# Key products of a recurrence round in four banks instead of two, and the last turn of outputs moved between two projections

## The reference

```
qkvz = einsum('bsd,od->bso', layernorm(x), W_qkvz)        # q, k, two v, two z for each of 16 heads
q, k, v = silu(causal_conv4(q, k, v)); q, k = rmsnorm(q), rmsnorm(k)
g = cumsum over the chunk; decay[i,j] = exp(g_i - g_j) for i >= j
M = where(i > j, einsum('cd,md->cm', k * beta, k) * decay, 0)
T = inverse(eye + M)                                      # 64 x 64, unit lower triangular
v_c, k_cumdecay = T @ (v * beta), T @ (k * beta * exp(g))
for each chunk:                                           # the recurrence
    attn  = (q @ k.T) * decay
    v_new = v_c - k_cumdecay @ state
    out   = (q * exp(g)) @ state + attn @ v_new
    state = state * exp(g_last) + (k * exp(g_last - g)).T @ v_new
h   = norm_w * rmsnorm(out) * silu(z)
s   = einsum('bsf,df->bsd', h, W_out)                     # summed over the heads
y   = x + s * silu(feed_forward(layernorm(x)))
```

## Time and profile before

| what | value |
|---|---|
| median of 3 runs | 2178.77 us (2178.72 to 2179.42) |
| profiled execution: its own time / its span | 2178.21 us / 2176.4 us |
| PE busy (matmul) | 2070.3 us, 95% of the span |
| DVE busy | 1597.4 us, 73% |
| POOL busy | 1670.5 us, 77% |
| ACT busy | 1192.7 us, 55% |
| chain that ended last | PE 49%, DVE 33%, ACT 9%, issue 6%, POOL 2% |
| granted TensorE clock, mean | 0.992 |

### The profile page before, as it was taken

The page is one execution under the profiler, slowest core; times in us unless marked ns, Lnnn a source line. Parts: engine busy times, 40 slices in busy tenths (PEclk is TensorE's granted clock), DMA queues, the critical chain, the costliest instruction groups (busy, mean ns, idle before and its releaser), DMA issues.

```text
span 2176.4 us, 75165 instructions
## 1 busy us (share of the span) xinstructions
PE 2070.3 (95%) x31952; PEld 1578.1 (73%) x31952; DVE 1597.4 (73%) x3083; ACT 1192.7 (55%) x2757; POOL 1670.5 (77%) x1774
## 2 busy tenths in 40 slices
PE   3799999999999999999999999999999999999998
PEld 2677777777777777777777777777777777776644
DVE  5777777778777777778777777778777777776322
ACT  3565556655665556655665556655665556654211
POOL 2788888888888888888888888888888888888200
PEclk9899999999999999999999999999999999999999
DMA  2211101111121101121121102111121102111100
GB/s 87 58 41 39 48 17 41 39 48 34 36 48 39 47 16 44 39 49 34 36 48 39 47 14 46 39 48 34 36 48 39 48 11 48 39 39 45 45 15 20
DMA packets 57485, 86.31 MB, mean 40 GB/s; under 512 B 7488, under 2 KB 30144, under 8 KB 57152
## 3 DMA queue, kind: packets, MB, share of 16 engines
q1 hardware_dynamic: 57152, 81.50, 15.2%
HBM read 76.92 MB, written 4.55 MB: 37 GB/s over the span
## 4 chain that ended last, share of the span: by engine, by line
PE 49%; DVE 33%; ACT 9%; issue 6%; POOL 2%; DMA 0%; DVEq 0%; POOLq 0%; SPq 0%; ACTq 0%
DVE cacc L1024 11%; PE ps_two L452 8%; PE ps_state L425 5%; PE ps_p L615 4%; DVE terms L1126 3%; PE ps_p L501 3%; ACT qg L799 3%; PE ps_state L639 3%; PE ps_p L680 3%; PE ps_p L623 3%; PE ps_p L588 3%; PE ps_p L452 2%; PE ps_p L739 2%; ACT L790 2%; PE ps_two L539 2%
## 5 line engine op out<-in xcount | busy, mean ns | idle before, releaser
L1411 POOL TENSOR_SCALAR Kg<-idx_s,lutb 128x134 f32<-128x134 int32 x480 | 356.3, 745 | 27.1
L1372 POOL TENSOR_TENSOR Sd<-St,el 128x512 f32<-128x512 f32 x192 | 201.3, 1048 | 196.9 <-DVEq L1266 196.9
L1245 DVE TENSOR_SCALAR Vn<-ps_p,bR 128x128 f32<-128x128 f32 x512 | 165.9, 349 | 189.8 <-PE ps_p L588 114.1
L425 PE MATMUL ps_two<-xnT,w_qkv 128*128 128x256 f32 x1024 | 235.7, 383 | 17.7 <-DVEq L1029 17.7
L1024 DVE SCALAR_TENSOR_TENSOR cacc<-ps_state,cw,cacc 128x1022 f32<-128x1022 f32 (+2 forms) x192 | 244.2, 1272 | 7.9 <-ACT cacc L772 3.1
L1024 DVE SCALAR_TENSOR_TENSOR cacc<-ps_two,cw,cacc 128x1022 f32<-128x1022 f32 (+2 forms) x192 | 244.8, 1275 | 5.3 <-DVE cacc L1024 0.5
L680 PE MATMUL ps_p<-w_o,hT 128*128 128x256 f32 x1000 | 242.4, 386 | 1.6 <-ACT V L835 1.6
L425 PE MATMUL ps_state<-xnT,w_qkv 128*128 128x256 f32 x1024 | 234.0, 382 | 5.9 <-DVEq L1029 5.9
L425 PEld LDWEIGHTS ps_two<-xnT,w_qkv 128*128 128x128 f32 x1024 | 190.3, 191 | 44.3 <-DVEq L1029 21.0
L425 PEld LDWEIGHTS ps_state<-xnT,w_qkv 128*128 128x128 f32 x1024 | 193.7, 192 | 32.3 <-DVEq L1029 6.3
L927 ACT ACTIVATE P<-ps_p 128x128 f32<-128x128 f32 x256 | 67.2, 277 | 267.7 <-PE ps_p L593 267.7
(11 more groups left out here) (192 smaller groups left out, 5014.4 us busy)
## 6 DMA issues: line engine op xcount, KB each, us to landing
qg<-g_scratch SPq DMA_DIRECT2D x64, 512.0 KB, 6.2
g_st<-g_scratch SPq DMA_DIRECT2D x64, 256.0 KB, 8.6
w_qkv<-in_wqkvz SPq DMA_DIRECT2D x16, 512.0 KB, 3.8
w_z<-in_wqkvz SPq DMA_DIRECT2D x16, 256.0 KB, 3.3
w_o<-in_wout SPq DMA_DIRECT2D x16, 256.0 KB, 2.9
idx_s<-in_idx SPq DMA_DIRECT2D x32, 67.0 KB, 1.9
fw_scratch<-looked_up SPq DMA_DIRECT2D x32, 67.0 KB, 2.7
Kg<-in_x SPq DMA_DIRECT2D x2, 1024.0 KB, 5.7
```

The lines of the kernel that those rows point to most:

```text
L425: m = pe.matmul(bank[:, t0:t0 + S // 2], w_qkv[:, k, kind * P:(kind + 1) * P], rows, start=(k == 0), stop=(k == KD - 1))
L1245: dve.tensor_scalar(Vn[:, cur, b], bank[:, 0:P], bR[:, R.par, b, c:c + 1], None, ALU.mult).then_inc(done, 1)
L1372: pool.tensor_tensor(Sd[:, :, :, :], St[:, c % 2, :, :, :], el[:, R.par, :, :, c].unsqueeze(3).broadcast_to([P, BB, RATIO, P]), ALU.mult). ...
L1411: m = pool.tensor_scalar(slots[k], idx_s[:, :], float(k), lutb[:, k:k + 1], ALU.is_equal, ALU.mult)
```

## The change

Two things are changed.

**Key products.** `begin` on PE fills four banks (4, 5, 6, 7) with two chunks each, where it filled two banks (4, 5) with four chunks each. DVE makes U in four operations of 2 x 2 x 64 columns instead of two of 2 x 4 x 64, and ACT copies `qk` in four pieces. The turned keys move to banks 4 and 5 (from 6 and 7) and so wait for the first two of these copies; the turned values move to banks 1, 6, 7, 4 (from 1, 4, 5, 7). Waits on the last key product now name number 3 instead of 1.

**Last turn of outputs.** On PE, `turn_back(R.before(), 3)` stands between projections 6 and 7 instead of ahead of both. On DVE, output part 2 (L1294) stands ahead of `gated(of, 3)` (L1285) instead of behind it. The last round keeps its order.

```diff
@@ -58,8 +58,8 @@
 def bank_uses(it):
 
     first, nxt = it == 0, it < ROUNDS - 1
-    begin = (spread([("kkq", i) for i in range(2)], (4, 5)) + spread([("kt", i) for i in range(2)], (6, 7))
-             + spread([("vt", i) for i in range(4)], (1, 4, 5, 7)))
+    begin = (spread([("kkq", i) for i in range(4)], (4, 5, 6, 7)) + spread([("kt", i) for i in range(2)], (4, 5))
+             + spread([("vt", i) for i in range(4)], (1, 6, 7, 4)))
     ahead = spread(PROJ, (0, 1, 6, 7)) if nxt else []
     outs = [] if first else spread([("out", 0), ("out", 1), ("out", 2), ("ot3", 0), ("out", 3)], (5, 4, 5, 4, 4) if nxt else (5, 4, 7, 4, 5))
     levels = []
@@ -494,12 +494,12 @@
             def begin(R):
 
                 pe.wait_ge(s["silu"], R.at(0, 4, 4))
-                for i in range(2):
+                for i in range(4):
                     bank, filled = wait_open(pe, R, "kkq", i)
-                    for u in range(4):
+                    for u in range(2):
                         for half in range(2):
-                            m = pe.matmul(bank[half * C:(half + 1) * C, u * P:(u + 1) * P], kq[:, i * 4 + u, 0, half, :],
-                                          kq[:, i * 4 + u, :, half, :], start=True, stop=True)
+                            m = pe.matmul(bank[half * C:(half + 1) * C, u * P:(u + 1) * P], kq[:, i * 2 + u, 0, half, :],
+                                          kq[:, i * 2 + u, :, half, :], start=True, stop=True)
                     m.then_inc(filled, 1)
                 for i in range(2):
                     bank, filled = wait_open(pe, R, "kt", i)
@@ -543,11 +543,14 @@
 
             def beside(R, lv, half):
 
-                if R.before() is not None and (lv, half) == (5, 1):
+                turn = R.before() is not None and (lv, half) == (5, 1)
+                if turn and not R.nxt:
                     turn_back(R.before(), 3)
                 if R.nxt:
                     for i in PROJ_AT.get((lv, half), ()):
                         proj(R, i)
+                        if turn and i == 6:
+                            turn_back(R.before(), 3)
                 else:
                     for f, j in GATE_UP_AT[lv, half]:
                         if f == 0 and j == 0:
@@ -813,11 +816,11 @@
                                ACT.Silu).then_inc(done, 1)
 
             def begin(R):
-                for i in range(2):
-                    act.wait_ge(s["u_c"], R.at(i + 1, 0, 2))
+                for i in range(4):
+                    act.wait_ge(s["u_c"], R.at(i + 1, 0, 4))
                     n, _ = R.use("kkq", i)
-                    src = ps[n][:, :].rearrange("p (c t) -> p c t", t=P)
-                    act.activation(qk[:, i * 4:i * 4 + 4, :], src[:, :, C:P], ACT.Copy).then_inc(read[n], 1)
+                    src = ps[n][:, 0:2 * P].rearrange("p (c t) -> p c t", t=P)
+                    act.activation(qk[:, i * 2:i * 2 + 2, :], src[:, :, C:P], ACT.Copy).then_inc(read[n], 1)
                 for i in range(2):
                     bank, done = wait_full(act, R, "kt", i)
                     act.activation(kt[:, i * 4:i * 4 + 4, :], bank[:, :].rearrange("p (c t) -> p c t", t=P), ACT.Copy
@@ -1081,13 +1084,13 @@
                 if last is not None:
                     gated(last, 2)
                 dve.wait_ge(s["dec_pool"], R.at(0, 7, 7))
-                for i in range(2):
+                for i in range(4):
                     bank, _ = wait_full(dve, R, "kkq", i)
-                    c4 = slice(i * 4, i * 4 + 4)
-                    src = bank[:, :].rearrange("p (c t) -> p c t", t=P)[:, :, 0:C]
-                    dve.tensor_tensor(U[:, :, c4, :], DB[:, :, c4, :], src.unsqueeze(1).broadcast_to([P, RATIO, 4, C]), ALU.mult
+                    c2 = slice(i * 2, i * 2 + 2)
+                    src = bank[:, 0:2 * P].rearrange("p (c t) -> p c t", t=P)[:, :, 0:C]
+                    dve.tensor_tensor(U[:, :, c2, :], DB[:, :, c2, :], src.unsqueeze(1).broadcast_to([P, RATIO, 2, C]), ALU.mult
                                       ).then_inc(s["u_c"], 1)
-                dve.wait_ge(s["u_c"], R.at(2, 0, 2))
+                dve.wait_ge(s["u_c"], R.at(4, 0, 4))
                 small_blocks(R)
 
             def small_blocks(R):
@@ -1216,10 +1219,10 @@
                 if R.nxt and of is not None:
                     outputs(R, "out", of, 1)
                 second_products(R, 5, 4)
+                if R.nxt and of is not None:
+                    outputs(R, "out", of, 2)
                 if of is not None:
                     gated(of, 3)
-                if R.nxt and of is not None:
-                    outputs(R, "out", of, 2)
                 if R.nxt:
                     taps(R, 2, (1, 2, 3))
                 else:
@@ -1357,8 +1360,8 @@
             def with_beta(R, b):
                 par = 0 if R.head else 1 - R.par
                 if not R.head and b == 0:
-                    wait_full(pool, R, "kkq", 1)
-                    pool.wait_ge(s["u_c"], R.at(2, 0, 2))
+                    wait_full(pool, R, "kkq", 3)
+                    pool.wait_ge(s["u_c"], R.at(4, 0, 4))
                 pool.wait_ge(s["dec_act"], R.at(2 * b + 1, 4, 4))
                 pool.wait_ge(s["n2_c"], R.at(4, 5, 5))
                 pool.tensor_tensor(DB[:, b, :, :], Dm[:, b, :, :], nbR[:, par, b, :].unsqueeze(2).broadcast_to([P, NC, C]),
...
```

More of the change, by code:

```diff
@@ L346, in body @@
                 if R.par == 1 and not R.nxt:
-                    wait_read(sp, R, "kkq", 1)
+                    wait_read(sp, R, "kkq", 3)
                     wait_read(sp, R, "kt", 1)
@@ L1438, in attention @@
                 for b in range(BB):
-                    wait_read(pool, R, "kkq", 1)
+                    wait_read(pool, R, "kkq", 3)
                     pool.tensor_tensor(A[:, b], qk[:, :, :], Dm[:, b], ALU.mult).then_inc(s["a_c"], 1)
```

## The result

The changed kernel is slower: a median of 2188.88 us (2187.28 to 2192.22, 6 runs) against 2178.99 us for the kernel before (6 runs), a ratio of 1.0046 with a 95% interval of 1.0033 to 1.0059. That is 9.9 us more, where 2188 us was forecast. The profiled execution has a span of 2186.8 us, 10.4 more than before. A round takes 61.62 us instead of 61.26: these are medians over the 31 distances between one round's transpose back to blocks (DVE) and the next.

The account below looks back on a forecast made before the run. PE bounds the kernel (59.95 of 61.32 us busy per round), with the chain of waits passing between DVE and PE; 16.2 lost minus 6.7 gained is 9.5 us more, from 2178.77 to 2188 us, range 2176 to 2197.

Parts of the forecast that it names:

- First edit, 0.21 us in each beginning: Key products in four banks: U whole 0.21 us earlier in each of 32 beginnings, 6.7 us gained.
- the third rival: The four U operations issue one by one, U no earlier; only the turn's move counts: 2195 us, chance 0.13.
- The rule of the Trainium skill: DVE's four U operations: small tiles each pay exposed access latency, so the gain would be nothing or a small loss.
- PE's room ahead of level 4: PE waits 11.2 / 32 = 0.35 us for DVE ahead of level 4's first products, enough to absorb a 0.1 us standstill.
- PE's gain of 0.36: At the end of level 5, projection 6 starts at 1082.99 where the turn started at 1083.35: PE gains 0.36 us.
- The turn 1.73 us behind projection 6: On PE the turn starts 1.73 us behind projection 6's start, making DVE's taps of kinds 2 and 3 0.60 us late.
- Room of 0.06 ahead of the recurrence: ACT's second key copy frees bank 5 0.08 us before batch 1's recurrence weights load; 0.06 us counted as slack.
- Gate 1's 0.32 of slack: Gate 1 on ACT frees bank 0 at 1095.96, PE's z part 3 starts at 1096.28: 0.32 us of slack.
- Rival (2): No difference: only gate 1 counts, 0.28 us per round, and the four banks give all 0.27; 2178.8 us, chance 0.14.
- 30 x 0.54 = 16.2 us lost: The moved turn delays the first recurrence products of batch 1 by 0.54 us in 30 rounds: 16.2 us lost.
- The faster one: DVE's gating is not late, so the taps keep their time and the four banks' gain remains: 2170.3 us, chance 0.17.

Follow-up runs that it names:

- experiment with the added operation: One more DVE operation of 256 columns, result unread, ahead of the taps of kind 2 in 30 rounds, on the kernel before; 2201.77 us, ratio 1.0109.
- the kernel in which it alone holds PE: The changed kernel with gate 2 on ACT put behind the two key copies of batch 0 instead of ahead; 2187.18 us, ratio 1.0035.
- The second edit alone: The kernel before with only the turn on PE and the gating on DVE moved, key products in two banks; 2197.26 us, ratio 1.0082.

## Why the prediction was right

The forecast was 9.5 us more, the result is 9.9. Its steps, one by one:

- *First edit, 0.21 us in each beginning.* U is whole 0.21 us earlier, the round alone is 0.19 shorter, and the first operation starts 0.22 us behind the gating, inside the bounds of 0.15 and 0.36; the start of before, which the third rival called unexplained, was DVE's wait for PE's first half (0.36 us). The turned keys are not held up by the copy that they newly need: they follow the last key product by 0.20 us in both kernels, and their weight load is idle for 0.17 us in both. The rule of the Trainium skill that was weighed there (VectorE: DVE Perf Modes, the TRN2 errata) did not set the price: the four operations take 1065.35 - 1063.94 = 1.41 us, where four full lengths of 0.417 are 1.67.
- *PE's room ahead of level 4.* This side reading was wrong: the 11.2 us of waiting are not 0.35 us in each round. The first and the last round have 3.6 and 2.6 of them and the 30 others 0.17 each, so PE had less room there than the prediction counted, and behind the edit this idle time is 0.04. The sum does not use it.
- *PE's gain of 0.36.* It was 0.35 at projection 6 and, by the median of the rounds, 0.23 at the start of keys_through (21.96 instead of 22.19 us behind the taps of kind 0), and none of it reached the recurrence.
- *The turn 1.73 us behind projection 6.* It started 1089.76 - 1087.93 = 1.83 us behind it, 0.10 more. The gating then started 1090.40 - 1089.76 = 0.64 behind the turn instead of 0.70, and the step to the taps was 0.15 as assumed. So the taps were 0.65 us late where 0.60 was worked out, and DVE's hole was 0.56 where 0.58 was worked out. That the turn of before had "long ended" ahead of the gating is too strong: it ended at 1083.35 + 0.63 = 1083.98, 0.24 us ahead; the sum does not rest on it.
- *Room of 0.06 ahead of the recurrence.* The delay is 0.65 and 0.57 arrives: 0.08. The experiment with the added operation gives 0.09.
- *Gate 1's 0.32 of slack.* Here the prediction was off, though its sum does not use it. z part 3 was 0.47 us late at a delay of 0.65, so the room at gate 1 was 0.18: the 0.32 leaves out the step of 1101.68 - (1100.96 + 0.58) = 0.14 us from gate 1's end (a gate takes 0.58) to PE's start. Gate 1 did most of the delay, the second copy the last 0.1. Rival (2), in which gate 1 alone counts, would not have come out as no difference: the kernel in which it alone holds PE is 7.0 us slower than before.
- *30 x 0.54 = 16.2 us lost.* The second edit alone lost 0.57 per round and 18.4 us in all. This term was some 1 to 2 us too small, for the late turn, and the first edit's was 1.3 too large (5.4 instead of 6.7); both misses lie within the measurement's interval. They go the same way: the two edits measured alone make 13.0. That the forecast lies within 0.4 us of the result is in part luck, since the interval of the 9.9 runs from 7 to 13 us; the path, the wait and the delay per round are what was shown.
- *The rivals.* The faster one needed the taps to be late by less than 0.27 us; they were 0.65 late. It was no strange case, though: with DVE's hole filled the change is faster, and by more than that rival gave.

What made it possible to be right was one reading: the chain of waits of before shows PE between 1083 and 1099, while the timelines of DVE and ACT show a second path, which ends at the first products of the recurrence with almost no room. An edit that gave PE 0.36 us and delayed that path by 0.6 had to lose.

## What to carry to other kernels

The chain that ended last is one path; before an operation is moved behind other work, look in the timelines for a path that ends at the same instruction with almost as little room, and count the delay there. Rounds that are late by chance can show that room before anything is changed. When a step goes behind a longer one on its producer, its consumer's whole list goes with it: put work that does not depend on it into the hole (here one tap of 1.3 us turned 1.0046 into 0.9954). Splitting a producer and its consumer into more pieces paid here, where the consumer's pieces follow each other closer than their own length (0.33 against 0.417 us for the operations of U) and the first one can start earlier.

## What the runs showed of the hardware

A DVE operation that reads two operands from SBUF, 128 x 256, took 0.59 to 0.94 us beside POOL's products, where the same kind with one operand in PSUM takes 0.417. In the lines above it started at 1097.52 under a POOL product that ended at 1098.18, and ended at 1098.46, 0.28 us behind that; POOL's next product took 2.08 us instead of the 1.90 of its neighbours. It ended 0.28 us behind POOL's product in each of the 30 rounds, whether it had started 0.66 or 0.31 us ahead of that end. The Trainium skill (SBUF — State Buffer, SBUF: two separate sides) says that DVE with two SBUF inputs and GpSimd take turns on a shared port pair, each holding it for a whole instruction; the trace agrees, in both directions. No run shows how long the operation takes without POOL beside it.

In the kernels with four banks a few rounds were longer by 0.2 to 0.4 us at the same places of the program (the 13th and the 16th of the 31 distances in each of them), with DVE waiting for POOL's scaled state for 0.76 instead of 0.41 us in the one that was looked at. The kernel before has such rounds at other places. Their cause was not tried and stays open; they are why the rounds' medians are compared here and not the totals alone.
